# A perceiver layer on one core: scores of two steps back to back, with the outputs between them

## The reference, cut to what matters

```python
lat = layer_norm(latents);  ctx = layer_norm(context)        # context: 16 batches x 1024 rows x 256
q = (lat @ Wq)                                               # 16 heads of 64
k, v = split(ctx @ Wkv)
k = apply_rope(k, cos, sin)                                  # x1*cos - x2*sin, x2*cos + x1*sin
attn = softmax(clip(q @ k.T * scale, -11, 11))
out = (attn @ v) @ Wo + bo
```

## Time and profile before

| | |
|---|---|
| time of three runs | 1238.22, 1241.43, 1241.9 us; median 1241.43 |
| the profiled execution | 1240.81 us, of them 1239.0 us from its first to its last instruction |
| mean granted clock of TensorE | 0.993 of full speed |
| PE busy | 1202.1 us |
| DVE busy | 1023.9 us |
| POOL busy | 709.3 us |
| ACT busy | 654.1 us |

### The profile page before, as it was taken

One profiled execution on the slowest core, in us unless ns is written; L12 is line 12 of the kernel. 1 busy time (PEld: TensorE's weight loads), 2 busy tenths in 40 slices (PEclk: granted clock), 3 DMA queues, 4 the chain that ended last, 5 costly groups with the idle time before them and its releaser, 6 DMA issues.

```text
span 1239.0 us, 39802 instructions
## 1 busy us (share of the span) xinstructions
PE 1202.1 (97%) x16268; PEld 997.0 (80%) x16268; DVE 1023.9 (83%) x1954; ACT 654.1 (53%) x1089; POOL 709.3 (57%) x611
## 2 busy tenths in 40 slices
PE   7899999999999999999999999999999899999997
PEld 3677887888888887888878887878878788899997
DVE  6699899998889889999899988899776266668886
ACT  7655555655545555555554555555433234356674
POOL 2467667777676766767667766667552033333332
PEclk9999999999999999999999999999999899999999
DMA  6256656556555655655555555555543540565662
GB/s 230 67 131 151 162 143 153 143 142 150 142 147 148 154 154 147 146 138 148 146 142 145 144 154 153 153 144 129 152 121 101 179 130 32 189 203 178 205 186 74
DMA packets 136173, 181.36 MB, mean 146 GB/s; under 512 B 30316, under 2 KB 96312, under 8 KB 135864
## 3 DMA queue, kind: packets, MB, share of 16 engines
q1 hardware_dynamic: 110552, 150.80, 45.1%
q10 hardware_dynamic: 21360, 23.80, 6.9%
q0 software_dynamic: 4080, 4.22, 1.7%
HBM read 81.93 MB, written 30.56 MB: 91 GB/s over the span
## 4 chain that ended last, share of the span: by engine, by line
PE 72%; DMA 7%; DVE 6%; SPq 6%; ACT 3%; POOL 3%; issue 3%; POOLq 0%; ACTq 0%; DVEq 0%
PE bank L1471 22%; PE bank L1499 20%; PE bank L1457 9%; PE bank L1807 6%; DMA ksw<-kw 4%; SPq L416 3%; POOL kr L566 2%; PE bank L1524 2%; PE bank L1635 2%; DVE kw L1046 2%; PE bank L1857 2%; PE bank L1858 2%; PE bank L1859 1%; SPq L408 1%; PE bank L1664 1%
## 5 line engine op out<-in xcount | busy, mean ns | idle before, releaser
L566 POOL TENSOR_TENSOR kr<-kr,ksw 128x1024 f32<-128x1024 f32 x128 | 308.6, 2411 | 290.0 <-DVE pr L1013 151.9
L1471 PE MATMUL bank<-ct,wk_hi 128*128 128x512 f32 x1024 | 332.0, 405 | 0.0
L1499 PE MATMUL bank<-p_hi,xc 128*128 128x512 f32 x1024 | 315.8, 390 | 0.0
L688 ACT ACTIVATE pr<-bank 128x1024 f32<-128x1024 f32 x128 | 131.4, 1026 | 322.4 <-PE bank L1457 321.0
L1499 PEld LDWEIGHTS bank<-p_hi,xc 128*128 128x128 f32 x1024 | 191.9, 188 | 39.9
L1471 PEld LDWEIGHTS bank<-ct,wk_hi 128*128 128x128 f32 x1024 | 182.9, 188 | 41.8 <-issue 0.3
L1471 PE MATMUL bank<-ct,wk_lo 128*128 128x512 f32 x512 | 201.4, 393 | 0.0
L1036 DVE TENSOR_TENSOR p_lo<-pr,p_hi 128x1024 fp32r<-128x1024 f32 x128 | 198.6, 1552 | 1.8 <-ACT p_hi L714 1.8
L1499 PE MATMUL bank<-p_lo,xc 128*128 128x512 f32 x512 | 199.1, 389 | 0.0
L1046 DVE TENSOR_TENSOR kw<-bank,stab 128x512 f32<-128x512 f32 x256 | 175.4, 685 | 3.5 <-PE bank L1471 2.4
L1457 PEld LDWEIGHTS bank<-qo,kr 64*64 64x64 f32 x8192 | 131.1, 134 | 54.9 <-issue 33.1
(11 more groups left out here) (219 smaller groups left out, 1682.3 us busy)
## 6 DMA issues: line engine op xcount, KB each, us to landing
ksw<-kw SPq DMA_DIRECT2D x512, 128.0 KB
x_turned<-xt SPq DMA_DIRECT2D x120, 128.0 KB
ctf<-x_turned SPq DMA_DIRECT2D x30, 512.0 KB
w_two<-in_L_ffn_W_dram SPq DMA_DIRECT2D x15, 1024.0 KB
raw<-in_ctx_dram ACTq DMA_DIRECT2D x56, 256.0 KB, 3.3
x_slots<-fill ACTq DMA_DIRECT2D x32, 258.0 KB, 2.7
w_all<-in_L_ffn_W_dram SPq DMA_DIRECT2D x4, 2048.0 KB, 17.5
wo<-in_L_ffn_W_dram SPq DMA_DIRECT2D x7, 1024.0 KB, 5.1
```

What stands on the lines that cost most here:

```text
L566: pool.tensor_tensor(kr[:, i], kr[:, i], ksw[:, i], ALU.add).then_inc(kr_done, 1)
L688: act.activation(pr_by_head, heads_by_tile, ACT.Exp, scale=SCALE).then_inc(exp_done, 1)
L1471: last = pe.matmul(psK[:, a * 512:(a + 1) * 512], l[:, k, w], ct[:, h % 3, r, k], start=(m == 0), stop=(m == len(parts) - 1))
L1499: last = pe.matmul(psZ[c], xc[:, slot_, l, t, cols], r[:, i, :, t], start=(f == 0 and m == 0), stop=(f == 1 and m == len(parts) - 1), skip ...
```

## The change

**On PE** two steps are taken together, j even: scores(j), the outputs of quad (j - 8) / 4 if j is a multiple of 4, scores(j + 1), keys(j + 3), sums(j - 2), keys(j + 4), sums(j - 1). **Banks:** even and odd steps have scores of their own (banks 2 and 3, 4 and 5), the sums move to 6 and 7, and the outputs go into the key banks 0 and 1. For this, outputs wait until the keys of step j + 2 are turned, and keys(j + 3) wait until DVE has added the outputs up and until the reciprocals are taken. **Keys** are made three steps ahead instead of two, with a third buffer `kr_third`, which takes the place of `ctf`; the turned context is loaded into the low half of `ct` itself. **Order on the others:** on DVE the addition of the outputs comes right behind the clamp, ahead of the keys; on SP the store of `x_turned` moves to another step of the quad. The opening and the last steps are written out anew for this order, and POOL prepares `vbd` later.

```diff
-        psZ, psT, psO = (bank[:, 4], bank[:, 6]), bank[:, 5], (bank[:, 5, D:D + 4 * N], bank[:, 7, 0:4 * N])
-        heads = bank[:, 2:4].rearrange("p h (t n) -> p h t n", n=N)
+        psZ, psT = (bank[:, 6], bank[:, 7]), bank[:, 5]
+        heads = (bank[:, 2:4], bank[:, 4:6])
...
+        def kr_at(j):
+            return kr_third[:] if j % 3 == 2 else kr[:, j % 3]
+        def out_bank(n, r):
+            return bank[:, r, 0:4 * N] if n < QUADS - 2 else (bank[:, 5, D:D + 4 * N], bank[:, 3, 0:4 * N])[r]
...
             def scores(j):
                 if there(j):
                     pe.wait_ge(kr_done, j + 1)
-                    wait(pe, exp_done, j)
+                    wait(pe, exp_done, j - 1)
...
+            def outputs(n):
+                pe.wait_ge(zt_done, 2 * n + 2)
+                wait(pe, o_sum, 2 * n)
+                if n < QUADS - 2:
+                    pe.wait_ge(ku_done, 8 * n + 22)
...
-            def step(j):
+            def two_steps(j):
                 scores(j)
-                outputs(j)
-                keys(j + 2)
+                if due(j, 8):
+                    outputs((j - 8) // 4)
+                scores(j + 1)
+                if due(j, 8) and there(j + 3):
+                    pe.wait_ge(o_sum, (j - 8) // 2 + 2)
+                keys(j + 3)
                 sums(j - 2)
+                keys(j + 4)
+                sums(j - 1)
...
             def step(j):
+                if due(j, 7):
+                    inverted((j - 7) // 4)
+                shifts(j)
+                counted(j)
                 clamped(j)
+                if due(j, 8):
+                    added((j - 8) // 4)
                 keys_turned(j, 0)
                 keys_turned(j, 1)
-                outputs(j)
                 weights_low(j)
                 blocks_turned(j)
-                divided(j)
-                context_low(j)
+                if due(j, 10):
+                    divided((j - 10) // 4)
+                if half_written(j - 2):
+                    half_low(half_written(j - 2))
```

More of the change, by code:

```diff
@@ L682, in biases, with sum_out, normalised, rows_high @@
                 act.copy(bias_rows[:], bank[0:DH, 4, :]).then_inc(bias_done, 1)
-            def step(j):
[L685 to L693, removed]
+            def sum_out(n, c):
+                act.wait_ge(z_ps, 4 * n + 3 + c)
+                wait(act, o_ps, n)
+                if n == 0:
+                    act.wait_ge(wv_done, 2)
+                if c == KC - 1:
+                    wait(act, lsum_ld, 64 * n - 48)
+                act.copy(zt[:, c], psZ[c]).then_inc(zt_done, 1)
+            def normalised(j):
+                for n in stats_at(j - 1):
+                    i = n % 2
+                    x_ = raw[:, n // ST % 2, n % ST]
+                    act.wait_ge(shift_done, n + 1 - ST)
+                    if n == ST:
                         act.wait_ge(xhat_done, ST)
                     act.activation(x_, x_, ACT.Identity, bias=shift[:, i:i + 1], scale=rstd[:, i:i + 1]).then_inc(xhat_done, 1)
[L696 to L712, removed]
-                    wait(act, z_ps, j // 2 * 2 - 2)
-                    act.copy(step_part(p_hi, j), pr[:]).then_inc(p_hi_done, 1)
+            def rows_high(j):
                 if there(j + 4):
@@ L834, in turned @@
                 act.copy(xnT[:, t % 2].rearrange("p k c -> p (k c)"), bank[:, 5, 0:D]).then_inc(xnT_done, 1)
[L836 removed]
+            for j in range(2, STEPS + 5):
                 step(j)
@@ L988, in counted @@
             def counted(j):
-                if ST <= j + 13 and there(j + 13):
-                    n = j + 13
+                for n in stats_at(j):
                     b, t = n // ST, n % ST
@@ L1238, in _ @@
             projected(0)
+            added(QUADS - 2)
+            normalise(0, 0)
+            divided(QUADS - 2)
+            inverted(QUADS - 1)
             projected(1)
-            normalise(0, 0)
-            divided(STEPS + 1)
-            outputs(STEPS + 3)
-            divided(STEPS + 5)
+            added(QUADS - 1)
+            divided(QUADS - 1)
             constants()
@@ L1645, in turn @@
                 last.then_inc(xnT_ps, 1)
-            for j in range(2, STEPS):
-                step(j)
-            step(STEPS)
+            for j in range(2, STEPS - 4, 2):
+                two_steps(j)
+            scores(STEPS - 4)
+            outputs(QUADS - 3)
+            scores(STEPS - 3)
+            pe.wait_ge(o_sum, 2 * QUADS - 4)
+            keys(STEPS - 1)
+            sums(STEPS - 6)
+            pe.wait_ge(ku_done, 2 * STEPS)
+            pe.wait_ge(vec2_ld, 32)
+            pe.transpose(bank[:, 1, 0:E * FT + 4], vec_rows2[:], ident[0:E * FT + 4, 0:E * FT + 4]).then_inc(tab_ps, 1)
+            weights_turned(0)
+            sums(STEPS - 5)
+            weights_turned(1)
+            weights_turned(2)
+            scores(STEPS - 2)
+            scores(STEPS - 1)
+            weights_turned(3)
+            weights_turned(4)
+            sums(STEPS - 4)
+            weights_turned(5)
+            weights_turned(6)
+            sums(STEPS - 3)
+            weights_turned(7)
+            pe.wait_ge(lw_done, 7)
+            project_heads(0, 0, PAIRS)
+            outputs(QUADS - 2)
+            sums(STEPS - 2)
+            pe.wait_ge(o_sum, 2 * QUADS - 2)
             turn(0)
-            step(STEPS + 1)
-            project_heads(2, 0, 2)
-            outputs(STEPS + 3)
-            project_heads(2, 2, 4)
+            sums(STEPS - 1)
+            project_heads(1, 0, PAIRS)
+            outputs(QUADS - 1)
+            project_heads(2, 0, 4)
             def keys_queries(t):
```

382 lines of the change are left out of this document (203 added, 179 removed).

## The result

The changed kernel takes 1271.09 us (median of four runs, 1269.13 to 1278.84) against 1240.62 us before (four runs, 1238.22 to 1241.9). The ratio is 1.026 with a 95% interval of 1.0213 to 1.0306: slower by 2.6%, where 0.8% less was forecast. The profiled execution took 1269.13 us. The time lies outside the forecast's range of 1218 to 1259 us.

The account below looks back on a forecast made before the run. PE, busy 97% of the span, was taken as the bound, with DVE to watch. From 1240.8 us, -20.7 -4.9 -1.8 +18.0 = -9.4 gave 1231 us, range 1218 to 1259 us.

Parts of the forecast that it names:

- What PE gains: On PE, less going over between large and small matmuls: 0.34 us less a pair, 20.7 us over 61 loop pairs.
- the sum: Whole kernel: -20.7 -4.9 -1.8 +18.0 = -9.4 us against the profiled 1240.8, rounded to 1231 us.
- the last rival: On PE, going over is not saved because the 0.2 us are semaphore waits: 1252 us; chance 0.02.
- The waits of scores for POOL: With keys three steps ahead, most should go: 4.9 us less in the window, 1.8 in the last steps.
- What is added: On PE, keys(j + 3) wait for the outputs' copy and addition in each of 30 quads: 18.0 us more.
- the keys' wait: Keys behind outputs wait for DVE's addition: 0.6 us a quad taken, floor 0.35, ends 0 and 1.4; 18.0 us.
- the hidden edits: Third key buffer, load into `ct`, moved store of `x_turned`, four score banks: taken as 0, with 3 us either way.
- Opening and end: Same matmuls in another order outside the loop: taken as 0, 3 us either way, beyond the 1.8 counted.
- DVE and POOL set the pace: Rival: further DVE waits go into the time, 1.4 us a quad, 42 us in all: 1255 us; chance 0.33.
- the signs of being wrong: In the profile: pairs shorter by under 0.2 us, keys' waits for DVE of 35 us up, or odd scores newly awaiting POOL.

Follow-up runs that it names:

- the second and third experiment: Changed kernel with shift and statistics behind the outputs' addition on DVE: 1268.71 us; changed kernel with SP's load of `lsum` back behind the swap: 1257.48 us.

## Why the prediction was wrong

**What PE gains: right.** A pair without outputs was said to fall from 13.52 to 13.18 us and measures 13.13; the pair with outputs is 14.06, against 14.11. 28 quads of 27.19 instead of 27.97 are 21.8 us less in the loop, where the sum had 19.0 for these 56 pairs. Sums ahead of keys and keys behind sums cost 2.72, as taken. The small error was in the last group of a row: scores that follow other small matmuls cost 1.04 us ahead of keys, as the outputs of the earlier trace rows did, and not 1.09. That also settles the last rival, by which the way over is not saved.

**The waits of scores for POOL: wrong in sign.** They were to go, -4.9 and -1.8. In the loop they became 11.3 us from 4.7. With the load behind the swap 2 are left: they came from the load, not from keys being three steps ahead.

**What is added: this is the step that failed.** The sum held one term for it, the keys' wait at 30 x 0.6 = 18.0 us, of which 16.8 fall on the 28 quads of the loop; it took the scores' waits as gone and the hidden edits as 0. The loop shows 63.6 us of waits and stops: 28.4 at the keys, 11.3 at scores and outputs, 15.4 of breaks, 8.5 of clock. So of the 46.8 us too little, 11.6 are the size of the term that was there, and the rest are terms that were put at nothing.

**The keys' wait: right mechanism, wrong size.** The text named this wait, its chain (swap, POOL's addition, `p_lo`, exponential, clamp) and its price for each size. It took 0.6 us a quad; the pairs give 1.0, and together with the breaks that lie in the same stretch keys start 4.59 us after the first scores (median) and not 3.6. The text followed one pair from an undisturbed start, and the lateness goes round. In the pair with outputs the swap landed 5.54 us after `kw`, not 4.7, so POOL's addition began 14.02 us into the pair and `p_lo` ended 1.4 into the next (these and the following are medians). In that next pair the swap was quicker than supposed, 4.36 in the mean, but its exponential and clamp had already started late (1.46 and 4.23), so `kw` was whole at 6.79 and not at 5.8, POOL added from 11.30 and not from 10.7, and the last `p_lo` again ended 1.44 into the pair with outputs, where 1.0 was taken. There the exponential started at 1.54 and the clamp, with the `shift` and the statistics ahead of it, at 3.30, where 2.28 was counted. The text had seen these two on DVE between `p_lo` and the clamp, but gave them no price of their own. One slip in it is small: a swap of 5.9 us makes the exponential 1.0 us late by its numbers, not 1.2.

**Hidden edits: wrong.** Of SP the text looked at the store of `x_turned` alone and took 0. The load of `lsum`, which the change moves ahead of the swap, was not looked at. Undone alone it gives 13.6 us, and with the keys freed of the addition 29.3 (1262.44 to 1233.18). The same edit costs nothing in the kernel before. So this move has no price of its own; it has the price of the slack behind it, which another part of the same change had used up.

**Not thought of at all:** the breaks in 192 small matmuls, 15.4 us in the loop, and the clock, 8.5 us. Neither is in any rival.

**The sum again**, for the loop: -21.8 for the work, +28.4 for the keys' wait, +6.6 for scores and outputs (11.3 less the 4.7 of before), +15.4 for the breaks, +8.5 for the clock make +37.1 of the +37.5 measured. Opening and end, taken as 0 with 3 us either way and -1.8 for a wait, gave -9.1; 3.4 of it is that the kernel before ran at the lower clock level from 980 to 987 us and this one did not. The rest of the -9.1 has no experiment.

**The rivals.** The slower one, DVE and POOL set the pace, was nearest: its sign and its chain are those of the trace, and its 1.4 us a quad would have given 1255. But it held that any further wait of DVE must go into the time, as if DVE's load were the bound. The kernel with outputs in score banks does the same work on DVE in 27.8 us a quad, where the changed one takes 29.5. So DVE's load was no bound; the order was. That its 42 us are near the wait and the breaks together (43.8) is chance, since it knew nothing of the breaks. Of the signs of being wrong one came: a new wait of odd scores for POOL, 10.6 of the 11.3 us. DVE's busy time rose by 13.0 us, where it was to stay or fall; `p_lo` takes 1612 ns in the mean, 1552 in the page before.

## What to carry to other kernels

When a change puts a new wait on the engine that is the bound, follow every queue that feeds the awaited work, and list each instruction that has moved ahead of it, on SP too; one that is free in the old order can be dear in the new one. When two causes feed one wait, undo both before judging either. And prefer a buffer whose next user comes late to one whose user comes next: with the load behind the swap in both, the outputs cost 22 us of waits in the key banks and none in the score banks behind the keys.

## What the runs showed of the hardware

**A long row of small matmuls breaks off where PE's instructions run out.** With 192 matmuls of 64 x 64 in a row (384 instructions of PE with their weight loads) PE stopped inside the last 64 at 10 to 14 places in every kernel that has such rows, by up to 2.5 us from start to start. In the kernels with rows of 128 at most there is one stop, of 0.2 us. The place is one in the program: the changed kernel and the second and third experiment stop after the same matmul of the same step (the 45th of step 29, the 29th of step 57, the 40th of step 69, the 52nd of step 81), whatever the other engines do then. The pages list the queue that brings instructions; here the changed kernel, the outputs computed twice, and the second copy behind the keys:

```profile
q8 instruction: 129, 2.11, 0.7%
...
q8 instruction: 145, 2.38, 0.8%
...
q8 instruction: 144, 2.36, 0.8%
```

A packet is 16 KB. The kernel before has 129 as well; 2048 more matmuls with their weight loads make 16 packets more, 1920 make 15. So q8 feeds PE, 256 instructions a packet. Now count all of PE's records in the traces, in order, from 0. In the six kernels with rows of 192 there are 69 stops, and each ends at a record whose number leaves 193 or 194 when divided by 256. Each time PE goes on 2.2 to 3.3 us after the start of a q8 packet, and the packet's number is always one less than the block's: the 14th packet for a stop in the 15th block of 256, the 100th for one in the 101st. The stop shown above ends at 467.69, and its packet started at 465.46. So PE stops at the border between two packets, for want of the next one. A border stops it only when it comes late in a row: in the changed kernel 15 borders fall into a third group, the ten that come behind its 24th matmul or later all stop, the five up to the 15th do not, nor do the 31 in a second group. What starts a packet, no run here shows.

**TensorE's clock falls behind such waits.** Windows of 1 us around the keys that start at 380.60, after 1.88 us of waiting for the addition:

```profile
379.00:380.00 1.00, 0.00 (x0) 0.00 (x0) 0.97 (x4) 0.68 (x2) 0.07 (x1) 1.00 1.21 195
380.00:381.00 1.00, 0.40 (x2) 0.36 (x3) 0.54 (x2) 0.76 (x1) 0.00 (x0) 1.00 0.74 242
381.00:382.00 1.00, 1.00 (x4) 0.81 (x3) 0.00 (x0) 0.60 (x2) 0.00 (x0) 0.50 0.81 274
```

The granted clock is 0.50 from 381 to 384.4, which is 1.2 GHz, and the large matmuls come every 0.43 us instead of 0.23. PE was idle through 379 to 380. The changed kernel has five such stretches of 3.4 us in the loop, at 115, 381, 715, 763 and 794 us, some 1.7 us lost in each. Each begins close to the end of a wait (0.4 us ahead of it to 1.4 behind), of 2.77, 1.88, 2.67, 2.17 and 1.92 us; waits of 1.86 and 2.65 us (at 145.71 and 498.35) were followed by none. Over the loops of all kernels here 15 of 31 waits of 1.8 us or more had such a stretch behind them. So a wait of 2 us may cost nearly 4. The Trainium skill (TensorE: Matmul & The Clock Gate, section on what's actually happening, its table of two states) has the lower level at 1.2 GHz after idle time. The rows show that level, behind idle time of 1.9 to 2.8 us.
